# Second mixture of experts gathered and summed by 0/1 products on the chip, and the folded output weights of the attention made earlier

## Reference

```python
# attention of layer 1: th1 mixes the heads' scores, th2 their probabilities
dots = einsum('gh,bhnm->bgnm', th1, dots); attn = softmax(dots)
attn = einsum('gh,bhnm->bgnm', th2, attn)
out = einsum('bhnm,bhmd->bhnd', attn, v) ...
h = h + out @ w_out + b_out
# mixture of layer 1: N = 32 experts, top 2, capacity C = ceil(1.25 * 1088 / 32) = 43
probs = softmax(x_flat @ Wg); vals, idx = top_k(probs, 2); vals = vals / vals.sum(-1)
pos = rank of this pick among all picks of its expert, in order of tokens
keep = pos < C; dest = where(keep, a * C + pos, N * C)
buf = zeros(N * C, D).at[dest].set(x_flat[token], mode='drop')
h1 = relu(einsum('ncd,ndh->nch', buf, W1) + b1)
o = (einsum('nch,nhd->ncd', h1, W2) + b2).reshape(N * C, D)
y = segment_sum(o[dest] * (vals * keep), token)
y = where(nothing kept, x_flat, y); h = h + y
```

## Time and profile before

| | us |
|---|---|
| median of 3 runs | 210.02 |
| lowest, highest | 209.72, 211.75 |
| span of the profiled execution | 214.1 |
| PE busy in it | 179.6 (84%) |
| DVE busy | 101.6 (47%) |
| ACT busy | 73.2 (34%) |
| POOL busy | 79.4 (37%) |

### The profile page before, as it was taken

The page is one execution under the profiler, slowest core; times in us unless marked ns, Lnnn a source line. Parts: engine busy times, 40 slices in busy tenths (PEclk is TensorE's granted clock), DMA queues, the critical chain, the costliest instruction groups (busy, mean ns, idle before and its releaser), DMA issues.

```text
span 214.1 us, 3836 instructions
## 1 busy us (share of the span) xinstructions
PE 179.6 (84%) x1347; PEld 135.6 (63%) x1351; DVE 101.6 (47%) x373; ACT 73.2 (34%) x219; POOL 79.4 (37%) x104
## 2 busy tenths in 40 slices
PE   6979799989899899999999889968787969986400
PEld 2946467777687699999687565457664436655200
DVE  0037676978453127882217618363446713333104
ACT  2002253543425445665510554083214002332100
POOL 8008341500875037886502300001156602565510
PEclk9995999996558999999999999979999985998855
DMA  6959999980121429981140179940011153111142
GB/s 183 291 156 307 367 294 346 368 350 5 36 52 26 101 57 318 301 327 40 37 119 4 48 225 428 318 112 0 3 33 37 38 118 48 42 34 35 32 124 53
DMA packets 18956, 31.12 MB, mean 145 GB/s; under 512 B 4838, under 2 KB 12517, under 8 KB 18554
## 3 DMA queue, kind: packets, MB, share of 16 engines
q1 hardware_dynamic: 15552, 27.15, 39.5%
q0 software_dynamic: 2784, 3.31, 6.0%
q10 hardware_dynamic: 602, 0.42, 0.7%
HBM read 23.52 MB, written 7.40 MB: 144 GB/s over the span
## 4 chain that ended last, share of the span: by engine, by line
PE 53%; POOL 12%; DMA 12%; issue 11%; DVE 5%; ACT 2%; SPq 2%; POOLq 1%; ACTq 0%; DVEq 0%
PE ps L1330 50%; POOL rooms L587 5%; DMA patchesT<-in_patchesT 4%; POOL rooms L549 4%; DMA xb<-rooms 2%; POOL o_rows L595 2%; DVE xn L866 2%; POOL ln_rstd L525 2%; PE ps L1788 1%; DMA o_tok<-o_rows 1%; DMA rooms<-xm,slot 1%; DMA rooms<-xm,room 1%; DMA o_rows<-o_sb,result_row 1%; SPq L411 1%; PE ps L1575 1%
## 5 line engine op out<-in xcount | busy, mean ns | idle before, releaser
L556 POOL DMA_INDIRECT o_rows<-o_sb,result_row x16 | 21.0, 1312 | 18.1 <-DVE o_sb L1073 15.7
L525 POOL TENSOR_TENSOR ln_rstd<-ln_var,minus_half 119x1 f32<-119x1 f32 x12 | 6.7, 566 | 51.3 <-DVE ln_var L860 51.3
L728 ACT ACTIVATE hid_b<-ps,w_ring 128x128 f32<-128x128 f32 x64 | 18.3, 369 | 14.2 <-PE ps L1330 13.4
L595 POOL DMA_INDIRECT o_rows<-o_sb,result_row x16 | 15.1, 943 | 18.7 <-DVE o_sb L1301 15.6
L549 POOL DMA_INDIRECT rooms<-xm,room x10 | 11.4, 1144 | 15.8 <-issue 15.8
L1330 PE MATMUL ps<-w_ring,hid_b 128*128 128x128 f32 x128 | 17.0, 276 | 0.3 <-ACT hid_b L728 0.3
L1330 PE MATMUL ps<-xbT,w_ring 128*128 128x128 f32 x128 | 17.0, 275 | 0.0
L1330 PE MATMUL ps<-filler 128*128 128x512 bf16 x51 | 15.4, 433 | 1.7 <-DVE filler L878 1.5
L824 ACT ACTIVATE hid<-ps,moe_b 128x64 f32<-128x64 f32 x32 | 8.3, 311 | 24.0 <-PE ps L1330 18.6
L1330 PEld LDWEIGHTS ps<-w_ring,hid_b 128*128 128x128 f32 x128 | 15.6, 192 | 0.5 <-ACT hid_b L728 0.5
L1330 PEld LDWEIGHTS ps<-xbT,w_ring 128*128 128x128 f32 x128 | 15.6, 192 | 0.0
(11 more groups left out here) (209 smaller groups left out, 361.8 us busy)
## 6 DMA issues: line engine op xcount, KB each, us to landing
w_ring<-in_w_routed SPq DMA_DIRECT2D x16, 514.0 KB
m<-in_m SPq DMA_DIRECT2D x2, 2048.0 KB, 13.0
rooms<-zeros SPq DMA_DIRECT2D x8, 330.0 KB, 5.4
patchesT<-in_patchesT SPq DMA_DIRECT2D x6, 272.0 KB, 5.3
xb<-rooms SPq DMA_DIRECT2D x16, 66.0 KB
w_s<-in_w_s SPq DMA_DIRECT2D x2, 512.0 KB, 5.9
moe_b<-in_moe_b SPq DMA_DIRECT2D x2, 512.0 KB, 16.9
rooms<-zeros SPq DMA_DIRECT2D x1, 792.0 KB, 6.7
```

The lines of the kernel that those rows point to most:

```text
L525: nc.gpsimd.tensor_tensor(ln_rstd[:, g:g + 1], ln_var[:, g:g + 1], minus_half[:], ALU.pow).then_inc(rstd_ready, 1)
L556: nc.gpsimd.indirect_dma_start(o_rows[:], bass.IndirectOffsetOnAxis(ap=result_row[:, b:b + 1], axis=0), o_sb[:, b, :], None).then_inc(o_sc ...
L595: nc.gpsimd.indirect_dma_start(o_rows[:], bass.IndirectOffsetOnAxis(ap=result_row2[0:past_, j:j + 1], axis=0), o2_sb[0:past_, j, :], None) ...
L728: nc.scalar.activation(hid_b[:, b % RING, c, :], ps[:, b % 2, c * BS:(c + 1) * BS], ACT.Gelu, bias=w_ring[:, b % WRING, FF + c:FF + c + 1] ...
```

## The change

*Folds.* `folded(0)` and `folded(1)` move from the attention to behind the shared up products, with PSUM banks 6 and 7 in place of 2 and 3, and their copies on ScalarE to before its work on the blocks. VectorE centres the weights and mixes the output weights before it makes the tables of the blocks.

*Gather.* Of a row's two picks only the sum `picked_at` of its two places is kept, and VectorE compares it with a constant table `slot_pos` of 32 x 44 slot numbers: `in_slot`, 119 x 1408 zeros and ones. The normed rows are split in two float32r tiles, `x_hi` (a cast on ScalarE) and `x_lo` (what is left over, on GpSimd), and six products per group (three banks, two parts) add the rows into their slots in PSUM, already transposed. VectorE and ScalarE copy the three banks to `x2T`; the experts work on 44 columns each, with the up products up to six pairs ahead.

*Sum.* A record of 16 floats for each pick (its token's number and its weight) is scattered to `rec_rows` and loaded to `rec_in`, 43 slots of each expert as rows. For pair j VectorE compares the token numbers 0 to 543 with the record (`of_token`, 128 x 544), ScalarE makes the weighed result's first part (`o2_hi`), VectorE the second (`o2_lo`), and four products add them to a transposed sum in PSUM banks 3 and 4, where a product with the identity adds h too. The output leaves transposed, in two DMAs; the host's code turns it.

*Beside these.* The rstd of all five groups is made on GpSimd by a power, the exponentials of the weights go by groups, the projection alternates between two banks, and the `filler` products of the router and before the experts are gone. The cut diff, in the order constants, GpSimd, ScalarE, VectorE, TensorE:

```diff
+RS = 44
...
+REC = 16
...
+GATHER_BANKS = (5, 6, 7)
+CRING = 3
+AHEAD = 6
+LATE = 4
...
+UP_BANK = (0, 1)
+DOWN_BANK = (2, 5)
+SUM_BANK = (3, 4)
+SPLIT = 2 * GT
...
+            def low_part(g):
+                n = rows(g)
+                pool.wait_ge(hi_ready, g + 1)
+                nc.gpsimd.tensor_tensor(x_lo[0:n, g, :], xm[0:n, g, 0, 0:D], x_hi[0:n, g, :].bitcast(F32),
+                                        ALU.subtract).then_inc(lo_ready, 1)
             def scatter2(g):
                 n = rows(g)
                 pool.wait_ge(slot_ready, g + 1)
-                pool.wait_ge(xn_ready, 3 * G + g + 1)
+                pool.wait_ge(weight_ready, g + 1)
                 for k in range(2):
-                    if k == 1:
-                        pool.wait_ge(xm_ready, G + g + 1)
                     nc.gpsimd.indirect_dma_start(
-                        rooms2[:], bass.IndirectOffsetOnAxis(ap=slot[0:n, g, k:k + 1], axis=0),
-                        xm[0:n, g, k, :], None).then_inc(scattered2, 16)
-            def spread_rows2(j):
-                past_ = ROOM + TAKEN
-                pool.wait_ge(o2_ready, j + 1)
-                nc.gpsimd.indirect_dma_start(
-                    o_rows[:], bass.IndirectOffsetOnAxis(ap=result_row2[0:past_, j:j + 1], axis=0),
-                    o2_sb[0:past_, j, :], None).then_inc(o2_scattered, 16)
-            pool.wait_ge(rooms2_zero, 16)
-            rstd(3, range(0, BY_POW))
-            for g in range(G):
-                scatter2(g)
-            for j in range(PAIRS):
-                spread_rows2(j)
+                        rec_rows[:], bass.IndirectOffsetOnAxis(ap=slot[0:n, g, k:k + 1], axis=0),
+                        rec[0:n, g, k, :], None).then_inc(scattered2, 16)
...
+            rstd(3, (0, 1))
+            low_part(0)
+            rstd(3, (2,))
+            scatter2(0)
...
+            def folded_out(half):
+                act.wait_ge(wf_done, half + 1)
+                nc.scalar.copy(w_f[:, 4 * half:4 * half + 4, :].rearrange("p g d -> p (g d)"),
+                               ps[:, 6 + half, :]).then_inc(wf_out, 1)
+            folded_out(0)
+            folded_out(1)
...
+            def result_high(j):
+                act.wait_ge(o2_ready, j + 1)
+                act.wait_ge(slot_w_ready, 1)
+                nc.scalar.activation(o2_hi[:, j, :], o2_sb[:, j, :], ACT.Copy,
+                                     scale=slot_w[:, j:j + 1]).then_inc(o2_hi_ready, 1)
+            for j in range(AHEAD):
+                rectified(j)
             for j in range(PAIRS):
-                rectified(j)
-            act.wait_ge(o2_scattered, 16 * PAIRS)
-            load_rest(act, o2_tok, o2_rest_loaded)
-            load_main(act, o2_tok, o2_loaded[1], 1)
-            load_main(act, o2_tok, o2_loaded[3], 3)
-            for g in (1, 3):
-                act.wait_ge(result_ready, g + 1)
-                act.dma_start(out[g * GT:g * GT + rows(g), :], ymoe[0:rows(g), g, :]).then_inc(stored, 16)
-            act.wait_ge(result_ready, G)
-            act.dma_start(out[LAST * GT + WHOLE_LAST:T, :], ymoe[WHOLE_LAST:rows(LAST), LAST, :]).then_inc(stored, 16)
+                if j + AHEAD < PAIRS:
+                    rectified(j + AHEAD)
+                result_high(j)
...
+            here(dve, "w_t", "th1_q", "th2_v", "w_out")
+            nc.vector.tensor_tensor(w_t[:, :, 0:D - 1], w_t[:, :, 0:D - 1], w_t[:, :, D - 1:D].to_broadcast([128, 12, D - 1]),
+                                    ALU.subtract).then_inc(w_centred, 1)
+            dve.wait_ge(w_centred, 1)
+            nc.vector.tensor_copy(w_t[:, :, D - 1:D], w_t[:, :, D:D + 1]).then_inc(w_centred, 1)
+            def out_weights(c):
+                nc.vector.tensor_tensor(out_mixed[:, c], w_out[:, c, :].unsqueeze(1).to_broadcast([128, H, D]),
+                                        th2_v[:, c, :].unsqueeze(2).to_broadcast([128, H, D]),
+                                        ALU.mult).then_inc(out_mixed_ready, 1)
+            dve.wait_ge(w_centred, 2)
+            for c in range(4):
+                out_weights(c)
...
+                nc.vector.tensor_tensor(in_slot[0:n, g % 2], slot_pos[0:n],
+                                        picked_at[0:n, g, :].unsqueeze(2).to_broadcast([n, EM, RS]),
+                                        ALU.is_equal).then_inc(in_slot_ready, 1)
...
+            def result_low(j):
+                dve.wait_ge(o2_hi_ready, j + 1)
+                nc.vector.scalar_tensor_tensor(o2_lo[:, j, :], o2_sb[:, j, :], slot_w[:, j:j + 1],
+                                               o2_hi[:, j, :].bitcast(F32), ALU.mult, ALU.subtract).then_inc(o2_lo_ready, 1)
+            def tokens_marked(j):
+                if j >= CRING:
+                    dve.wait_ge(summed, j - CRING + 1)
+                nc.vector.tensor_scalar(of_token[:, j % CRING, :], token_no[:], rec_in[:, j, 0:1], None,
+                                        ALU.is_equal).then_inc(of_token_ready, 1)
...
+                if j + LATE < PAIRS:
+                    pair_biased(j + LATE)
+                tokens_marked(j)
+                result_low(j)
...
+            folded(0)
+            folded(1)
...
-            folded(0)
             pe.wait_ge(keys_out, 2 * H)
             dots(2)
             dots(3)
-            folded(1)
             pe.wait_ge(xq_loaded, 16 * PER)
             pe.wait_ge(dots_read, BATCHES)
             held(0)
-            pe.wait_ge(wf_out, 2)
             held(1)
             project(0)
             held(2)
             project(1)
             held(3)
             router_turn(0)
-            fill(1, 3)
             router_logits(0)
             project(2)
             slot_ranks(0)
             router_turn(1)
-            fill(1, 3)
             router_logits(1)
             project(3)
             slot_ranks(1)
+            gather(0)
...
+                for i, bank in enumerate(GATHER_BANKS):
+                    own = slice(i * BANK_OF_EXPERTS, min((i + 1) * BANK_OF_EXPERTS, EM))
+                    width = (own.stop - own.start) * RS
+                    for part in (x_hi, x_lo):
+                        last = mm(ps[:, bank, 0:width], part[0:n, g, :],
+                                  in_slot[0:n, g % 2, own, :].rearrange("p e r -> p (e r)"),
+                                  g == 0 and part is x_hi, g == G - 1 and part is x_lo)
...
-            fill(FILLS, 6)
...
+            def pair_summed(j):
+                pe.wait_ge(of_token_ready, j + 1)
+                pe.wait_ge(o2_hi_ready, j + 1)
+                for i, own in enumerate((slice(0, SPLIT), slice(SPLIT, T))):
+                    for part in (o2_hi, o2_lo):
+                        if part is o2_lo and i == 0:
+                            pe.wait_ge(o2_lo_ready, j + 1)
+                        last = nc.tensor.matmul(ps[:, SUM_BANK[i], 0:own.stop - own.start], part[:, j, :],
+                                                of_token[:, j % CRING, own], start=j == 0 and part is o2_hi,
+                                                stop=j == PAIRS - 1 and part is o2_lo)
...
+                if j + AHEAD - 2 < PAIRS:
+                    pair_down(j + AHEAD - 2)
+                if j + AHEAD < PAIRS:
+                    pair_up(j + AHEAD)
+                pair_summed(j)
+                if 1 <= j <= G:
+                    residual(j - 1)
```

431 lines of the change are left out of this document (248 added, 183 removed).

## The result

| | before | changed |
|---|---|---|
| median | 210.17 us | 239.82 us |
| lowest, highest | 209.72, 211.75 | 237.49, 241.94 |
| span of the profiled execution | 214.1 | 238.8 |

The ratio is **1.136**, with an interval of 1.127 to 1.145: slower by 29.7 us at the median. I had said 230, with 207 to 238. The direction and the mechanism came out as forecast, the size did not: the time lies 1.8 us above the range.

A forecast was written before the change was run, and what follows sets the result against it. TensorE was taken to bind up to the router, then scatter, reload and expert pairs. On the trace, 172.0 + 56.5 for the experts + 5.6 for the folds gave 234.1, +20.0, so 230 us at the median; range 207 to 238.

The forecast's parts named there:

- The closed round: Loop over pairs: each iteration waits on all three engines in turn, 3.4 us at half clock, 2.5 at full clock.
- The clock: Expert loop: 1.2 GHz before the experts start, since the router loop leaves TensorE little work; the round would not restore it.
- the dear product: Rival, sums: float32r products cost half of float32's price, 244 us, or its full price, 273 us; chance 0.09.
- The folds: Folded output weights moved early: +5.6 us before the routed stage, -3.9 us in the attention.
- The attention's fall to half clock: Rival, attention stage: half clock for want of the folds, 2 to 3 us more; counted within the forecast's 0.52.
- The router: First join to last slots: 26.3 us instead of 21.6, +4.7, with VectorE the bound at about 5.0 us a group.
- The gather: Last slots to the experts' first up product: 4.0 us instead of 8.1, -4.1 us.
- the four terms ahead of it: Changes before the experts start: folds +5.6, attention -3.9, router +4.7, last slots to first up product -4.1 us.
- The carry from the trace to the median: Whole kernel: span 214.1 is 4.1 us over the median 210.02; the span's difference was carried to the median unchanged.
- The faster one: Rival, loop over pairs: the round doesn't close, TensorE's 1.3 us a pair sets the pace, 202 us; chance 0.14.
- The full clock with a closed round: Rival, loop over pairs: full clock holds, 214 us, give or take 3; chance 0.25.
- The records: Scatter, wait and load: 7.6 us after the comparison, covered by seven up and five down products unless these take longer.

The follow-up runs named there:

- e1: Changed kernel with the sum of pair j-1 issued in iteration j, behind the up products of j+6; 224.09 us, ratio 1.066.
- e11: Changed kernel with ScalarE making the high part of pair j before it rectifies pair j+6; 229.04 us, ratio 1.093.
- e2: Changed kernel with fillers behind the last three logits, in the last two rounds before the sums, and three in each iteration; 231.89 us, ratio 1.102.
- e3: e1 with the fillers of e2 ahead of the loop, but one filler instead of three in each iteration; 227.53 us.
- e5: e1 with fillers behind the last three logits, around the last gather and in four rounds before the sums, none in the loop; 210.19 us, ratio 0.988.
- e7: e5 with the folds, their copies and VectorE's centring and mixing back at their old places; 204.76 us, ratio 0.970.
- e8: e7 without the late sum: the sum of pair j is back in its own iteration; 235.86 us, ratio 1.121.
- e10: e7 with 3, 1 and 1 fillers in place of 5, 3 and 3 around the last gather and before the sums; 207.65 us, ratio 0.986.
- e4: The kernel before with only the folds, their copies and VectorE's centring and mixing moved as in the change; 214.42 us, ratio 1.013.
- e12: The kernel before with six more fillers ahead of the reload and three behind the first pair's up products; 209.35 us, ratio 0.997.

## Why the prediction was wrong

**The closed round: right in kind, too cheap.** It was the heart of the forecast, with the links that e1 and e11 each opened. The term was 3.4 us and measured 3.98. In the forecast's own steps (from the rows of the round at 188 to 193 and the one before it): down products 0.6, measured 0.62; up products to ScalarE's start 0.9, measured 1.12; two relus, high part, low part and hand-overs 1.2, measured 1.26; rest of the sum 0.7, measured 0.98. **The step that failed is the price of TensorE's own short products in the round**, 0.5 of the 0.58 us. Two prices were wrong.

The up products were priced below the row of 128 columns for having 44. They take 1.08 us where those of 128 took 1.06: the columns do not matter here. Each record has a load of weights of its own, 0.93 us for the four, and that did not shrink. The Trainium skill (TensorE: Matmul & The Clock Gate, Back-to-back issue gap) says that in a stream of load and product the distance is set by both; for the up products the trace agrees.

The rest of the sum was priced by its columns alone. In a row of sums the columns do give the price, with 0.20 and 0.22 us behind the products of 238 at the end of the changed kernel:

```profile
232.05 0.40 PE L1920 MATMUL ps<-of_token,o_hi 128*128 128x238 f32 x1
...
232.25 0.42 PE L1920 MATMUL ps<-of_token,o_lo 128*128 128x238 f32 x1
...
232.47 0.47 PE L1920 MATMUL ps<-of_token,o_hi 128*128 128x306 f32 x1
```

In a round the second product is followed after 0.32 instead (191.82 to 192.14), and the fourth by the down products after 0.39 (188.43 to 188.82). e1, which waits for nothing, has 0.22 and 0.38 there: the 0.32 goes with the wait for the low part, the 0.39 does not. Why the change from sum to down products costs more than the columns stays open.

The loop's 5.7 us too many (62.2 for 56.5) are 5.2 in the nine rounds with their residuals, 0.9 up to the end of the first sum (put at 11.3, though its parts, at the forecast's own prices, add up to 10.3), and 0.4 less behind them.

**The clock: right.** 1.2 GHz was forecast before the experts start, and it was there from 168 on. Of the first reason, the thin router, the runs show part: with two fillers behind each of the last three logits the clock still fell behind 172 in e2 and e3; with fillers around the last gather and ahead of the loop too, e5, e7, e8 and e10 reached the loop at 1.00. The second, that the round itself doesn't feed the clock, was the better one: e8 lost it within two rounds. But e1 shows that a round without waits didn't raise it either.

**float32r: right.** Products of 306 columns lie 0.27 us apart at 1.2 GHz, one pass; the dear product did not come.

**The folds: +5.2 for +5.6, and -3.0 for -3.9.** e4 gives +6.0 and -2.9. The attention's fall to half clock, one of the rivals, was there (0.50 from 140 to 142), but the kernel before and e12 fall in the same place with the folds still there. **The router: +6.0 for +4.7.** The comparison takes 1.62 us as priced at 1.6, and the joins of the middle groups are 5.0 us apart (153.04 to 158.05); but VectorE is busy for only 19.4 of 27.4 us, so it is not nearly full, as I had it. TensorE is at half clock from 152 to 156 and from 168 on. In e7, at full clock, the same stretch takes 24.96, +3.6, so the forecast's price for the work was too dear and the clock, which it had not counted in the router, made it too cheap. **The gather: -3.9 for -4.1**, right.

**The experts' start: right by luck.** 176.6 for 177.6 hides two misses: the four terms ahead of it were 2.0 us too cheap in sum (+4.3 for +2.3), and the stretch ahead of the shared up products, which the forecast put at nothing, came 3.1 us shorter.

**The carry from the trace to the median: wrong, and nearly as dear as the round.** The forecast of the median was 9.8 us off: 5.7 from the loop, 1.0 less for the earlier start of the experts, and 5.1 from the carry. Of these, 1.0 is the distance from the traced span, 238.8, to the median, and 4.1 are what I took off as an offset between span and median. It was none: in the timed runs of all kernels the time is the span plus 1.8 to 2.3 us, and the timed executions of the kernel before have spans of 205.7 to 212.6. The traced one, 214.1 at a mean clock of 0.886, was simply long: its loop of 38.75 us held two stretches at half clock, and e12's is 32.8. That excess lay in the very stretch which the change replaces, so it could not be taken off the changed kernel. A forecast span of 234.1 was a forecast of about 236 us.

**The rivals.** The faster one, an open round, is what e7 built by hand: 202.5 in span and 204.8 at the median, where I had worked out 205.8 and 202. That the numbers are close is in part luck: e7 has late folds, a round of 1.5 and not 1.3, and the 3 us at its start. The full clock with a closed round (214) did not occur: e8 entered its loop at 1.00 and lost it, and at 2.4 GHz the round is 2.85 in e2, with fillers in its wait, not 2.5. The records came in time: the first sum, at 187.50, waited for the high part, as the later ones do.

## What to carry to other kernels

A lookahead in the loop's indices is worth nothing if each engine still ends an iteration with a step that another engine needs in the same iteration; walk the cycle through all engines' queues, and let the consumer lag by one. Price a short product by a row of one that is equally short and has the same neighbours, not by its columns. Before a traced execution is compared with a median, ask whether its own clock was that of the others: two executions of one kernel here are 8 us apart. And before a stretch is held to be the gain, cut both traces at the same events from the first instruction to the last: of the 4.9 us between e12 and e7, 0.8 lie in the part that was rewritten for it.

## What the runs showed of the hardware

**A busy TensorE can stay at half clock.** In e1 it is busy in the profile for all of 29 us and the granted clock is 0.50 throughout; in e7, and in e5, which differs from e1 only in fillers ahead of the loop and the bank of one turn, the same rounds are reached at 1.00 and keep it (in e7 1.00 up to TensorE's last product). These rounds ran at either clock, and the runs differ in what went before them. The Trainium skill (TensorE: Matmul & The Clock Gate, What's actually happening) says that activity releases the throttle; busy rows in the trace were not enough here.

**GpSimd is slower while VectorE compares.** The power on GpSimd takes 0.59 us alone and 2.04 beside a comparison in the changed kernel (first fence); in e7 a scatter's issue takes 2.28 us beside it and 1.08 alone (second fence).

```profile
159.43 0.59 POOL L547 TENSOR_TENSOR ln_rstd<-ln_var,minus_half 119x1 f32<-119x1 f32 x1
...
164.48 2.04 POOL L547 TENSOR_TENSOR ln_rstd<-ln_var,minus_half 119x1 f32<-119x1 f32 x1
164.50 1.61 DVE L1281 TENSOR_TENSOR in_slot<-slot_pos,picked_at 119x1408 fp32r<-119x1408 f32 x1
```

```profile
162.71 1.62 DVE L1279 TENSOR_TENSOR in_slot<-slot_pos,picked_at 119x1408 fp32r<-119x1408 f32 x1
...
163.00 2.28 POOL L617 DMA_INDIRECT rec_rows<-rec,slot  x1 [0.31 <-DVE rec L1295]
...
168.98 1.08 POOL L617 DMA_INDIRECT rec_rows<-rec,slot  x1 [0.30 <-issue]
```

The Trainium skill (Advanced Engine Details and Errata, GPSIMD Details) says that the two share a read and a write interface and conflict when a VectorE instruction has two inputs in SBUF; the comparison has, and the traces agree. No run here moved the comparison elsewhere, so what this costs the router was not measured.
